# Initial fills of the key and value buffers, the w1 weights and the row copies of the first tile, in a macaron layer kernel

## The reference

```python
x = x + 0.5 * ffn(layernorm(x))          # the same k0, k1, k2 both times
x = x + attn(layernorm(x))               # 16 heads of 8, softmax over 256 keys,
                                         # then layernorm(ctx + input) * gamma + beta
x = x + 0.5 * ffn(layernorm(x))
# ffn: h = s0 * [x, -x] @ sign(k0); h = 2 relu(h)
#      h = s1 * h @ sign(k1);       h = 2 relu(h);   h = s2 * h @ sign(k2)
# k0: 256 x 512, k1: 512 x 512, k2: 512 x 128, booleans read as +1 or -1
```

## Time and profile before

| | |
|---|---|
| median of 3 runs | 983.64 us (979.5 to 984.24) |
| span of the profiled execution | 983.6 us |
| what lies around the span | nothing that the two figures can tell apart |
| PE busy | 87% of the span |
| DVE busy | 74% |
| ACT busy | 58% |
| POOL busy | 35% |
| PE busy in the first 70 us | 40.28 us |
| PE busy from 300 to 600 us | 274.45 us |

### The profile page before, as it was taken

The page is one execution under the profiler, slowest core; times in us unless marked ns, Lnnn a source line. Parts: engine busy times, 40 slices in busy tenths (PEclk is TensorE's granted clock), DMA queues, the critical chain, the costliest instruction groups (busy, mean ns, idle before and its releaser), DMA issues. The chain is left out here.

```text
span 983.6 us, 21936 instructions
## 1 busy us (share of the span) xinstructions
PE 857.4 (87%) x7258; PEld 357.5 (36%) x7258; DVE 724.8 (74%) x1610; ACT 566.0 (58%) x995; POOL 339.9 (35%) x471
## 2 busy tenths in 40 slices
PE   6559799999799997999979998899979999878885
PEld 2223324344333433434334343334334444233332
DVE  5646878979668785778859797789858788777633
ACT  2123666666456664656646665567656676666742
POOL 4430142525224241433415253243415343242331
PEclk8786979999979888879979999889979899797988
DMA  2000000010101001010100101010010101010000
GB/s 56 12 33 19 27 17 30 21 37 19 40 2 37 20 26 33 8 38 13 37 22 18 40 13 40 9 35 22 29 31 13 44 12 34 3 34 13 13 1 21
DMA packets 28768, 23.88 MB, mean 24 GB/s; under 512 B 5616, under 2 KB 28656, under 8 KB 28656
## 3 DMA queue, kind: packets, MB, share of 16 engines
q1 hardware_dynamic: 28656, 22.37, 7.2%
HBM read 5.05 MB, written 4.19 MB: 9 GB/s over the span
## 5 line engine op out<-in xcount | busy, mean ns | idle before, releaser
L799 ACT ACTIVATE probs<-ps_t,score_scale 128x512 f32<-128x512 f32 x512 | 344.4, 685 | 184.4 <-PE ps_t L644 184.1
L1015 DVE TENSOR_REDUCE row_max<-ps_s 128x2 f32<-128x512 f32 x512 | 345.0, 685 | 100.3 <-PE ps_s L630 97.1
L767 ACT ACTIVATE ffn_hi<-ps_z 128x512 f16<-128x512 f32 x288 | 171.5, 596 | 143.9 <-PE ps_z L557 75.5
L966 DVE SCALAR_TENSOR_TENSOR ffn_lo<-ps_z,ffn_hi 128x512 f16<-128x512 f32 x256 | 176.3, 689 | 105.4 <-ACT ffn_hi L767 99.8
L630 PE MATMUL ps_s<-k_rows,q_rows 24*128 24x256 f16 x1024 | 198.8, 293 | 32.7 <-issue 14.4
L644 PE MATMUL ps_t<-q_rows,k_rows 26*128 26x256 f16 x1024 | 197.0, 291 | 24.5 <-issue 13.0
L556 PE MATMUL ps_z<-ffn_hi,w 128*128 128x512 f16 x512 | 200.8, 392 | 11.9 <-DVE ffn_lo L966 11.9
L557 PE MATMUL ps_z<-ffn_lo,w 128*128 128x512 f16 x512 | 198.1, 387 | 0.0
L664 PE MATMUL ps_c<-probs,v_cols 128*32 128x256 f32 x2048 | 155.5, 426 | 0.1
L630 PEld LDWEIGHTS ps_s<-k_rows,q_rows 24*128 24x128 f16 x1024 | 53.4, 94 | 188.5 <-issue 97.3
L452 POOL TENSOR_TENSOR att_ve<-att_mv,eps 128x4 f32<-128x4 f32 x16 | 3.2, 201 | 289.1 <-DVE att_mv L949 289.1
(11 more groups left out here) (113 smaller groups left out, 1035.8 us busy)
## 6 DMA issues: line engine op xcount, KB each, us to landing
x<-L_attn_x SPq DMA_DIRECT2D x16, 256.0 KB, 2.8
q_rows<-q_hi SPq DMA_DIRECT2D x128, 32.0 KB
k_rows<-k_hi SPq DMA_DIRECT2D x128, 32.0 KB
q_rows<-max_rows SPq DMA_DIRECT2D x256, 2.0 KB
y<-x SPq DMA_DIRECT2D x16, 256.0 KB, 2.1
q_rows<-q_lo SPq DMA_DIRECT2D x64, 32.0 KB
k_rows<-k_lo SPq DMA_DIRECT2D x64, 32.0 KB
k_raw<-L_ffn_k SPq DMA_DIRECT2D x1, 256.0 KB, 3.4
```

The lines of the kernel that those rows point to most:

```text
L767: a_.activation(ffn_hi[:, use, :], ps_z[use % 2][:], ACT.Relu if use else ACT.Copy, scale=1.0 if use else XN_SCALE).then_inc(z_hi, 1)
L799: a_.activation(probs[grp % 2][:, softmax_lane(u), :], ps_t[u % 2][:], ACT.Exp, scale=score_scale[:, 0:1]).then_inc(s_exp, 1)
L966: v.scalar_tensor_tensor(out=ffn_lo[:, use, :], in0=ps_z[use % 2][:], scalar=0.0, in1=ffn_hi[:, use, :], op0=ALU.max, op1=ALU.subtract).th ...
L1015: v.tensor_reduce(row_max[u // HB % 2][:, j::LANES, g % 2], ps_s[u % 2][:].rearrange("p (a k) -> p a k", a=2), AX.X, ALU.max).then_inc(s_m ...
```

## The change

The fills are split up. POOL fills `k_rows[0]` right behind its constants, ahead of the first normalisation. DVE fills `v_cols[0]` and its ones columns as its very first work. POOL fills `k_rows[1]` and `v_cols[1]` behind `att_norm(0, 0)`. New semaphores, one for each buffer, take the place of `CONSTS`. ACT does the use-0 split of the first FFN ahead of w1, and PE waits for w1 only at piece 6, where w1 is first read. The 12 copies of k are issued on ACT's queue, four each behind the splits of pieces 7, 8 and 9 of the second FFN (piece 9 has none); the 12 of q stay on SP.

```diff
+        s_vfill = [sem(f"v_cols{i}_filled") for i in range(2)]
+        s_kfill = [sem(f"k_rows{i}_filled") for i in range(2)]
@@ SP
             spread(0, 0, SPREADS // 2)
-            sp.wait_ge(m_free, 3)
-            sp.wait_ge(s_const, CONSTS)
-            spread(0, SPREADS // 2, SPREADS)
+            sp.wait_ge(s_kfill[1], 1)
@@ POOL
             last.then_inc(s_const, 1)
+            g.memset(k_rows[0][:], -1.0 / M_UNIT).then_inc(s_kfill[0], 1)
...
             g.partition_all_reduce(w_most[:], w_inv[:], P, RMAX).then_inc(s_setp, 1)
-            for i in range(2):
-                g.memset(k_rows[i][:], -1.0 / M_UNIT).then_inc(s_const, 1)
-                g.memset(v_cols[i][:], 0.0).then_inc(s_const, 1)
-            pool.wait_ge(s_const, CONSTS - 2)
-            for i in range(2):
-                g.memset(v_cols[i][:, :, :, HD:HD + 1], 1.0).then_inc(s_const, 1)
             ffn_norm(1, x3)
             att_norm(0, 0)
+            g.memset(k_rows[1][:], -1.0 / M_UNIT).then_inc(s_kfill[1], 1)
+            g.memset(v_cols[1][:], 0.0).then_inc(s_vfill[1], 1)
+            pool.wait_ge(s_vfill[1], 1)
+            g.memset(v_cols[1][:, :, :, HD:HD + 1], 1.0).then_inc(s_vfill[1], 1)
@@ PE
                 if s == 1:
                     pe.wait_ge(s_setd, SETD_FFN)
+                elif s == FFN_MID[0][0]:
                     pe.wait_ge(s_w1, 1)
@@ ACT
+            ffn_piece(0, 0)
             act.wait_ge(s_setd, SETD_W0)
             a_.activation(w1[:], k1_raw[:], ACT.Identity, ...).then_inc(s_w1, 1)
-            for s in range(16):
+            for s in range(1, 16):
                 ffn_piece(0, s)
@@ ACT, second FFN
                 elif what == "V":
-                    act.wait_ge(s_const, CONSTS)
+                    act.wait_ge(s_vfill[0], 2)
                     v_copy(0, 0, 3)
+                elif s == 7:
+                    act.wait_ge(m_free, 3)
+                    act.wait_ge(s_kfill[0], 1)
+                if s in (7, 8, 9):
+                    for j in range(LANES):
+                        part = s - 7
+                        a_.dma_start(k_rows[0][ROWS * j + HD * part:ROWS * j + HD * (part + 1), :, :],
+                                     (qk_lo if part == 1 else qk_hi)[1][ROWS * j:ROWS * (j + 1), :]).then_inc(s_spread, 16)
+            act.wait_ge(s_vfill[1], 2)
@@ DVE
+            v.memset(v_cols[0][:], 0.0).then_inc(s_vfill[0], 1)
+            dve.wait_ge(s_vfill[0], 1)
+            v.memset(v_cols[0][:, :, :, HD:HD + 1], 1.0).then_inc(s_vfill[0], 1)
             dve.wait_ge(s_x0, 16)
             ffn_stats(x0)
```

More of the change, by code:

```diff
@@ L259, in run @@
                 steps(it)
-        CONST_IDENT, CONST_NORM, CONSTS = 4, 8, 14
+        CONST_IDENT, CONST_NORM = 4, 8
         SETD_W0, SETD_FFN, SETD_SQUARES, SETD_BOUND, SETD_FIT, SETD_ALL = 7, 11, 13, 15, 19, 24
```

## The result

The changed kernel takes 972.28 us in the median of 17 runs (963.72 to 981.08), beside 983.64 us for the kernel before (17 runs, 976.1 to 997.59). The ratio is 0.9881, with a 95% interval from 0.9846 to 0.9916: faster by 11.7 us, or between 8.3 and 15.1 us. The forecast was 973.5 us, 10.1 us faster. Both kernels spread by over 1% from run to run, so the parts of the change have to be read from the head of the profile and not from the times. The ratio leaves out the runs that lie over 1.5% above the fastest of their kernel, and the profiled execution, 978.99 us with a span of 976.8, is one of those. In the runs here the time lies about 2 us above the core's span; the table ahead of the prediction doesn't show this, and it changes no difference.

The account below looks back on a forecast made before the run. POOL's fills stalling DVE, and so PE, were taken to bound the head, with PE's wait for k copies. Tile 0's residual 10.5 us earlier, less 0.4 for ACT's queue, gave 10.1: 983.6 to 973.5 us, range 967.5 to 978.5.

Parts of the forecast that it names:

- The stall of DVE: First FFN: POOL's fills hold DVE's operation on 3 columns for 8.68 us; without them it lasts 0.2 us.
- The head up to the residual of tile 0: First FFN: third block starts near 22.1 and takes about 1.9 us; residual at 28.8 instead of 39.34, 10.5 us earlier.
- POOL: Behind the all-reduce: gap of 7.5 us, tile 1 normalised from 26.8; late fills cost nothing, at most 4.8 us.
- The copies on ACT: Second FFN: issues of 0.70 us hold ACT's splits; tile 1's residual 3.9 us late, 0.4 us of the gain lost.
- The first iteration and the end: After the head: its saving of 10.1 us should reach the end one for one; transposes near 61.3.
- (1): Copies in second FFN: an issue costs ACT nearly nothing; gain 14 us, time 969.6; chance 0.17.
- (2): Copies in second FFN: SP and ACT take turns at one resource; gain 5.8 us, time 977.8; chance 0.10.
- (3): Head: third block stays at the lower clock or DVE's opening fill holds POOL's first fills; 975.2 to 976; chance 0.15.
- (4): Copies on ACT: slower by over 0.5% from an issue price of 1.95 us; chance 0.07 over 1.2, 0.03 beyond 1.95.
- (5): First FFN: the gap behind the all-reduce, not the fills, holds L916; gain about 3 us, time 980.5; chance 0.03.

Follow-up runs that it names:

- the second profile of the changed kernel: The changed kernel run and profiled again, nothing altered, beside the kernel before: ratio 0.9943 (0.9899 to 0.9987).
- the kernel with the gaps: Changed kernel with five k copies on SP and seven on ACT, between and behind splits: ratio to the kernel before 0.9842, in the second set 0.9775.

## Why the prediction was right

**The stall of DVE.** Right, and shown: 8.68, 4.34 and 0.17 us for two, one and no pair of fills behind the all-reduce.

**The head up to the residual of tile 0.** Forecast 28.8, measured 28.00. The third block started at 21.43 (forecast 22.1) and took 1.94 us (forecast 1.9). I had let PE's second block set that start. In this profile the block was over by 19.5 and DVE's remainder, which ended at 21.38, set it, because PE's clock, granted at 0.86 on average in the first 20 us before, was granted in full there after.

```profile
0.00:20.00 20.00, 12.32 (x44) 4.50 (x44) 11.79 (x33) 7.10 (x9) 8.45 (x22) 1.00 0.34 69
20.00:40.00 20.00, 13.20 (x85) 7.45 (x86) 11.96 (x37) 6.23 (x12) 11.01 (x11) 0.91 0.04 14
```

These are two windows of the changed kernel: the stretch and its length, busy time of PE, its weight loads, DVE, ACT and POOL, and then the granted clock. PE's wait ahead of its first product of the FFN went from 3.27 to 1.51 us, but this is not what kept the clock up: the seven other profiles with the early fills and w1 moved have the same wait, 1.50 or 1.51 us, and a granted clock of 0.83 to 0.91 over the same 20 us. In the second profile of the changed kernel (0.85) PE's second block does set the start of the third, at 22.12, as forecast. The 0.7 us are chance of one execution.

**POOL.** The second gap was 6.87 us and not 7.53, and tile 1's normalisation began at 26.31 (forecast 26.8). The late fills held nothing: DVE's remainders beside them took 0.69 and 0.68 us, as everywhere.

**The copies on ACT.** The mechanism was right, ACT stands while it issues, and the price of 0.70 us was right: 0.68 each. The loss was mis-sized, and it is the one term of the sum that was far off. I let the residual of tile 1 come 3.9 us late; behind the use-5 split it came 6.1 us late in this profile (13.31 us against 7.22) and 7.1 in the second. Three things were missing from that term. The first issue took 1.35 instead of 0.7 us, and with the steps between, the last two splits started at 52.65 and not at 51.8. I carried over the 2.04 us from the last split to the residual, though the output products of the earlier blocks, which used to run under the splits, now start behind both: they ran from 54.02 to 56.4, and the residual came 3.9 us behind the start of the two splits. And behind its wait of 3.86 us PE ran part of these products at the lower clock: from the first of them to the residual it took 2.24 us before, 2.52 here and 3.48 in the second profile. At the transposes the forecast had the copies cost 0.4 us, and they cost 2.6 and 3.6.

**The first iteration and the end.** I had the transposes at 61.3, and they came at 62.25, so the head gained 9.1 us there and not 10.1. At the first maximum of tile 1's scores the lead was 11.7 us in the trace, and 6.8 at the end of it. In between it rose to 13.8, fell to 4.7 and rose again to 12.4, by the starts of DVE's residuals, in iterations whose code is the same in both kernels. That the head's saving is handed on one for one is therefore not shown. The interval of the ratio, 8.3 to 15.1 us, holds the head's 9.1; the 22 us of the kernel with the gaps in its second set, against 13.4 in its head, do not fit it. The forecast stands 1.2 us from the median, within an interval of 3.4 us to either side; it can't be said to be better than that. It is also in part luck. In the head two errors stood against each other: 0.8 to 1.2 us more gain ahead of the copies, and 2.2 us more loss by them. The head then gained 9.1 us, and the 2.6 us from there to the 11.7 of the ratio have no term in the sum.

**The rivals.** *An issue costs ACT nothing* (1) fell: the hole of 5.16 us is there. *Taking turns at one resource* (2) fell: SP's last four issues of q ran from 44.54 to 47.33 beside ACT's, and took 2.79 us, as the same four did in the kernel before with ACT silent. The rule of the Trainium skill that I put beside it, Perfetto Trace Analysis (DMA Instruction, HWDGE), has the generator locked for exclusive use by each issue. This trace does not agree: with both queues issuing at once SP's took 2.79 us as without ACT, ACT's took 0.68 us each but for its first, and the measurement decides. (3) did not occur: the constants of POOL stayed at their times beside DVE's fill, and the third block ran at the upper clock (1.00 from 21.4 to 25.3). (4) fell with the price of 0.68. (5) fell with the 0.17 us of the operation inside the gap, and with the second pair put back.

## What to carry to other kernels

Work that one engine does "some time at the start" is free only if it holds up no other engine's short operation: look for an instruction on few columns that lasts as long as another engine's fills (8.68 us on 3 columns here). A DMA issue moved to a compute engine's queue, 0.68 us on ACT here, keeps that engine's next instruction from starting. So count the issues against the time from the start of one of its instructions to the start of the next: four in a row cost the FFN more than the second queue gained, one in each 1.73 us cost nothing and made the way from the use-5 split to the transposes 6.1 to 7.1 us shorter than the change had it. Where the times of one program spread by over 1% and the marks in its profiles by 2 us, measure a part over a stretch that begins right ahead of it: the same one repeated here to 0.02 us.

## What the runs showed that I had not expected

DVE's fill of 128 x 3072 f32 took 2.62 us, 0.85 ns a column, less than my lower bound of 2.73 and far from the 3.2 us that I took. It started at 1.46 instead of 0.7, so the end, 4.08, was near my 4.3 by luck.

Short holds between DVE and POOL go both ways. In the changed kernel POOL's ffn_xn took 1.35 us instead of 1.04, while DVE was at work on w_diff, and DVE's operation on w took 1.01 instead of 0.35 while POOL worked on ffn_xn. The second is off the path. The first is not: PE waited 0.38 us for ffn_xn ahead of its transposes at 9.22. In the other kernels with DVE's fill at the start ffn_xn took 1.35 to 1.56 us, and with that fill moved it took 1.04.

The first DMA issue on ACT took 1.29 to 1.35 us and the later ones 0.68 to 0.75, whether SP was issuing beside it or not.
